# Turning the packed token statistics on VectorE before they are broadcast, in a 16-batch fused embedding and MLP kernel

## The chip, the cores and the metric

The kernel runs on one core of one Trainium2 chip. The metric is the device time of one execution in microseconds; lower is better. One execution was also taken with the hardware profiler, and all rows below are from it.

## The reference

For each of 16 batches, `x` holds 512 tokens of 512 features. Six variants of `x` are built, weighted and concatenated to 3072 features, and go through a two-layer MLP with a layer norm, and the result is added to `x`:

```python
h = _ln(x, pw_g[pathway_ids], pw_b[pathway_ids])
h = _ln(h, cp_g[compartment_ids], cp_b[compartment_ids])
t = _ln(x, tm_g[time_steps], tm_b[time_steps])
m, n, r = (x + _mlp_ln(state_i, ...)[:, None, :] for three state vectors)
s = _ln(x, ms_g[scale_type], ms_b[scale_type])
cat = concatenate([w[0]*h, w[1]*t, w[2]*m, w[3]*n, w[4]*r, w[5]*s], -1)
out = x + _ln(silu(cat @ int_W1 + int_b1) @ int_W2 + int_b2, int_g, int_be)
```

`_ln` normalises over the 512 features of a token. So each token needs its mean and its reciprocal deviation before `t` and `s` can be made.

## The kernel before

All matmuls are exact to about fp32: each operand is split in a high and a low part of type fp32r, and three products (lines 1325 to 1327) are summed in `hid_ps`. Features lie on the partitions and the 512 tokens of a batch in the free dimension: `xc` is `[128, 4, 512]`, transposed `x`. The 16 batches run as `chunk(0)` to `chunk(15)`; chunks 2 to 14 are one hardware loop. The order of the work on each engine is written out by hand, and the engines meet at semaphores.

The statistics of batch b+1 are made while batch b is multiplied. In `x_stats` VectorE takes mean and variance of each token with tokens on the partitions (`xmv`). GpSimd's `x_rstd` turns the variance into the reciprocal deviation, splits it in two fp32r parts and writes `x_pack` `[128 partitions, 2 parts v, 2 statistics s, 4 tokens t]` (lines 452 to 462). The partition p and the number t name the token. But for `t` and `s` the same statistics are needed along the free dimension, on every partition. SyncE's `spread_stats` does this through DRAM: one DMA writes `x_pack` to `token_stats` (line 340), SyncE waits until it has landed, and two DMAs read it back, each to 64 partitions, into `stats_bc` `[128, p, s, t]` (line 347, the first and the second broadcast below). Batch 0 does not use this path; it spreads its statistics with TensorE.

VectorE then uses `stats_bc` in two instructions a batch: `scaled_next` (line 840) multiplies a one-hot mask with the deviations, and `centre` (line 805) subtracts the mean from `xc`. Both read one float in eight: the elements of one statistic are 32 bytes apart.

```python
mean = stats_bc[:, :, 0, :].rearrange("q p t -> q t p").unsqueeze(1).to_broadcast([P, FT, TT, P])
```

TensorE multiplies `scaled` with class tables in `fill(b, j)` (line 1305, into `made_ps`), VectorE multiplies the result with `xc` in `ts_mult(b, j)` (line 854, into `v_ring`), ScalarE and VectorE split that (`ts_high`, `ts_low`, line 859), and TensorE multiplies it with the weights. `fill(b, 0)` waits for `scaled`; `fill(b, 1)` waits for `ts_mult(b, 0)`, as there is one `made_ps`.

The hand-written order of VectorE at the end of a chunk matters here. In chunks 2 to 15 it is: `h_low(b,0)` (line 864), `out_sum(b-1,2)` (line 952), `x_low(b+1,0)` (line 792), `h_low(b,1)`, `out_stats(b-1,3)` (line 904 ff.), `onehot_next`, `scaled_next(b+1)`, two `y_mul` (line 872), `out_sum(b-1,3)`, `x_low(b+1,1)`, `centre(b+1)`, two `y_add` (line 878 ff.), two `y_norm` (line 890), and then `ts_mult(b+1,0)`. In chunk 1 the tail begins with `h_low(1,1)`, `out_sum(0,1)`, `x_low(2,0)`, `out_sum(0,2)`. In chunk 0 it is `y_mul(1,0)`, `y_mul(1,1)`, `add_b1`, `centre(1)`, `scaled_next(1)`, `y_add(1,0)`. `y_norm(b,t)` also needs class rows, which GpSimd gathers with `gather_class(b,t)` (line 490) after `y_mul(b,t)`. SyncE's queue holds, behind `spread_stats(b+1)`, the stores of batch b-1 and the next loads.

Of the kernel before, what the change touches and what calls it, by code (L numbers as in the profile page):

```python
# [7 lines left out]
BATCHES, TOKENS, D = 16, 512, 512  # L8
P = 128
TT = TOKENS // P  # L10
FT = D // P
# [23 lines left out]
def build(nc, x, xT, ids, pid, small, small_at, tm_g, ms_g, rows, net_vecs, pw, cp, W1s, W2s, int_W1, int_W2, out):  # L35
# [4 lines left out]

    x_v = x.rearrange("b (p t) d -> b p t d", t=TT)
    out_v = out.rearrange("b (p t) d -> b p t d", t=TT)
    stats_dram = nc.dram_tensor("token_stats", (2, P, 2 * TT), f32, kind="Internal").ap()

    with ExitStack() as ctx:
        def sb(name, shape, dt=f32):
            return ctx.enter_context(nc.sbuf_tensor(name, shape, dt))

        def sem(name):
            return ctx.enter_context(nc.semaphore(name))  # L50
# [2 lines left out]
        y_sb = sb("y_sb", [P, TT, D])  # L53
        pw_rows = sb("pw_rows", [P, TT, 2 * D])
        xc = sb("xc", [P, FT, TOKENS])
        stats_bc = sb("stats_bc", [P, P, 2, TT])
        r_sb = sb("r_sb", [P, TT, D])
        cat_hi = sb("cat_hi", [P, SLOTS, 2, TOKENS], f32r)
        with ExitStack() as before:
# [49 lines left out]
        xmv = sb("xmv", [P, TT, 2])  # L109
        xve = sb("xve", [P, TT])  # L110
        xrs = sb("xrs", [P, TT])
        x_pack = sb("x_pack", [P, 2, 2, TT])
        split = sb("split", [P, 2, TT])
        split_by = sb("split_by", [P, TT])
        yst = sb("yst", [P, TT, 6])
# [98 lines left out]
        xrs_done = sem("xrs_done")  # L214
        xsplit = sem("xsplit")
        x_packed = sem("x_packed")
        sel_ready = sem("sel_ready")
        mean_diag = sem("mean_diag")
        dev_diag = sem("dev_diag")
# [49 lines left out]
        def wait(eng, s, value):  # L269

            if not isinstance(value, int) or value > 0:
                eng.wait_ge(s, value)
# [40 lines left out]
        def _(sp):  # L313
# [22 lines left out]
                                 ).then_inc((sum_in if j == 0 else sum_more_in)[k], 16)  # L336

            def spread_stats(b):
                sp.wait_ge(x_packed, 4 * b + 2)
                sp.dma_start(stats_dram.rearrange("v p m -> p v m"),  # L340
                             x_pack[:, :, :, :].rearrange("p v s t -> p v (s t)")).then_inc(stats_out, 16)
                sp.wait_ge(stats_out, 16 * b)

                wait(sp, centred, FT * b)
                wait(sp, scaled_ready, b)
                for v in range(2):
                    sp.dma_start(stats_bc[64 * v:64 * v + 64, :, :, :].rearrange("q p s t -> q (p s t)"),
                                 stats_dram[v].rearrange("p m -> (p m)").partition_broadcast(64)
                                 ).then_inc(stats_in[v], 16)

            def store(b, t):
# [82 lines left out]
        def _(pool):  # L434
# [6 lines left out]
            def x_rstd(b):  # L441

                if isinstance(b, int) and b == 1:
                    pool.wait_ge(dev_diag, 1)
                    pool.wait_ge(rest_diag, 1)
                else:
                    wait(pool, stats_out, 16 * (b - 1))
                rstd(xaggr, TT * (b + 1), xve, xve_done, xrs, xrs_done, xmv, slice(0, TT), b + 1)
                pool.nop(nofuse=True)
                if not (isinstance(b, int) and b == 0):  # L450

                    pool.tensor_copy(x_pack[:, 0, 0, :], xmv[:, :, 0]).then_inc(x_packed, 1)
                    pool.tensor_copy(x_pack[:, 1, 0, :], xmv[:, :, 0]).then_inc(x_packed, 1)

                pool.wait_ge(xrs_done, b + 1)
                pool.tensor_tensor(split[:, 0, :], xrs[:, :], split_by[:, :], ALU.mult).then_inc(xsplit, 1)
                pool.wait_ge(xsplit, 2 * b + 1)
                pool.tensor_tensor(split[:, 1, :], split[:, 0, :], xrs[:, :], ALU.subtract).then_inc(xsplit, 1)
                pool.wait_ge(xsplit, 2 * b + 2)
                pool.tensor_tensor(x_pack[:, 0, 1, :], split[:, 0, :], split[:, 1, :], ALU.subtract).then_inc(x_packed, 1)  # L460
                pool.wait_ge(x_packed, 4 * b + 1)
                pool.tensor_tensor(x_pack[:, 1, 1, :], xrs[:, :], x_pack[:, 0, 1, :], ALU.subtract).then_inc(x_packed, 1)
# [52 lines left out]
            pool.memset(minus_half[:, :], -0.5).then_inc(half_ready, 1)  # L515
            pool.memset(eps_col[:, :], EPS).then_inc(half_ready, 1)
            pool.memset(split_by[:, :], 4097.0).then_inc(half_ready, 1)
            pool.memset(net_hidT[:, :, :], 0.0).then_inc(cols_cleared, 1)
            pool.memset(mT[:, :, :], 0.0).then_inc(cols_cleared, 1)
            pool.memset(cat_lo[:, 3, 0, 0:P // 2].bitcast(f32), 1.0).then_inc(sel_ready, 1)  # L520
            pool.memset(cat_lo[:, 3, 0, P // 2:P + P // 2].bitcast(f32), 0.0).then_inc(sel_ready, 1)
            pool.memset(cat_lo[:, 3, 0, P + P // 2:2 * P].bitcast(f32), 1.0).then_inc(sel_ready, 1)
            pool.wait_ge(cols_cleared, 3)
            pool.wait_ge(half_ready, 3)
            pool.wait_ge(sel_ready, 4)
            x_rstd(0)
            pool.wait_ge(row_ids_in, 16)
# [248 lines left out]
        def _(dve):  # L776
# [13 lines left out]
            def x_low(b, i):  # L790
                dve.wait_ge(x_hi_done, 2 * b + i + 1)
                dve.tensor_tensor(cat_lo[:, slot(i), :, :], xc[:, 2 * i:2 * i + 2, :],
                                  cat_hi[:, slot(i), :, :].bitcast(f32), ALU.subtract).then_inc(x_lo_done, 1)

            def stats_here(b):
                for v in range(2):
                    dve.wait_ge(stats_in[v], 16 * b)

            def centre(b):

                dve.wait_ge(x_lo_done, 2 * (b + 1))
                stats_here(b)
                mean = stats_bc[:, :, 0, :].rearrange("q p t -> q t p").unsqueeze(1).to_broadcast([P, FT, TT, P])
                v = xc[:, :, :].rearrange("q f (t p) -> q f t p", t=TT)
                dve.tensor_tensor(v, v, mean, ALU.subtract).then_inc(centred, FT)  # L805

            def centre_tile(f):

# [28 lines left out]
            def scaled_next(b):  # L837
                stats_here(b)
                wait(dve, filled, 6 * (b - 1) + FT)
                dve.scalar_tensor_tensor(scaled[:, :].rearrange("q (t p) -> q t p", t=TT),  # L840
                                         ids_sb[:, :].rearrange("q (t p) -> q t p", t=TT), cls_val[:, 0:1],
                                         stats_bc[:, :, 1, :].rearrange("q p t -> q t p"),
                                         ALU.is_equal, ALU.mult).then_inc(scaled_ready, 1)

            def ts_mult(b, j):
# [210 lines left out]
            def first_chunk():  # L1056
                class_columns()
                x_low(0, 0)
                sum_blocks(0)
                x_stats(0, 0)  # L1060
                sum_low(0)
                x_stats(0, 1)
                x_stats(0, 2)
                x_stats(0, 3)
                sum_blocks(1)
                tab_low()
                sum_low(1)
                x_low(0, 1)
                sum_blocks(2)
                dev_diagonal()  # L1070
                sum_low(2)
                sum_blocks(3)
                scaled_first()
                sum_low(3)
                centre_tile(0)
                ts_mult(0, 0)
                w_low(4)
                w_low(5)
                centre_tile(1)
                ts_low(0, 0)  # L1080
                ts_mult(0, 1)
                w_low(6)
                w_low(7)
                centre_tile(2)
                ts_low(0, 1)
                onehot_first()
                centre_tile(3)
                w_low(8)
                w_low(9)

                dve.wait_ge(tables_ready, 1)
                y_mul(0, 0)
                y_mul(0, 1)
                ts_mult(0, 2)
                y_mul(0, 2)
                y_mul(0, 3)
                ts_low(0, 2)
                w_low(10)
                w_low(11)
                y_add(0, 0)  # L1100
                ts_mult(0, 3)
                y_add(0, 1)
                ts_low(0, 3)
                y_add(0, 2)
                y_add(0, 3)
                w_low(12)
                for t in range(TT):
                    y_norm(0, t)
                w_low(13)
                nets_stats()  # L1110
                h_low(0, 0)
                w_low(14)
                w_low(15)
                x_stats(1, 0)
                h_low(0, 1)
                nets_norm()
                class_rows()
                for t in range(1, TT):
                    x_stats(1, t)
                x_low(1, 0)  # L1120
                nets_weigh()
                x_low(1, 1)
                onehot_next(1)
                y_mul(1, 0)
                y_mul(1, 1)
                add_b1()
                centre(1)
                scaled_next(1)
                y_add(1, 0)

            def chunk(b, last=False):
                if isinstance(b, int) and b == 1:
# [31 lines left out]
                    out_stats(b - 1, 2, o_ps[:, 0, :])  # L1164
                    h_low(b, 1)
                    out_sum(b - 1, 1)
                    x_low(b + 1, 0)
                    out_sum(b - 1, 2)
                else:
# [25 lines left out]
                    out_sum(b - 1, 1)  # L1195
                    out_stats(b - 1, 2, o_ps[:, 0, :])
                    h_low(b, 0)
                    out_sum(b - 1, 2)
                    if not last:
                        x_low(b + 1, 0)  # L1200
# [428 lines left out]
```

## Time and profile before

| | |
|---|---|
| median of 3 runs | 995.85 us (994.02 to 996.64) |
| the profiled execution | 994.5 us, span 992.8 us |
| TensorE busy | 98% of the span |
| VectorE busy | 81% |
| GpSimd busy | 51% |
| ScalarE busy | 27% |
| mean granted TensorE clock | 0.995 |

The span runs from the first to the last instruction; some 1.7 us of the execution lie around it. Busy shares are averages over stages. For a kernel with TensorE at 98% the short list of what TensorE waited for is the first thing to read, and then what stands behind each of these waits.

### The profile page before, as it was taken

What the parts mean: (1) busy time and instruction counts of PE and PEld (TensorE: products, weight loads), DVE (VectorE), ACT (ScalarE), POOL (GpSimd) and SP (SyncE); (2) the same over time, 40 slices, a digit from 0 to 9 for tenths busy, and PEclk for the clock granted to TensorE, in tenths of its full rate; (3) what the DMA queues carried; (4) which work ended last, traced back from release to release, by engine and by line L of the source; (5) the groups of instructions that cost most, each with busy time, mean ns of one, the idle gap of its engine ahead of it and who ended that gap; (6) DMA issues with size and microseconds to landing.
All of it is one profiled execution on the core that took longest, in us unless ns stands there. A gap on an engine that the chain in (4) does not pass through costs nothing.

```text
span 992.8 us, 13724 instructions
## 1 busy us (share of the span) xinstructions
PE 976.8 (98%) x4436; PEld 802.4 (81%) x4436; DVE 800.0 (81%) x1102; ACT 272.1 (27%) x341; POOL 505.4 (51%) x624
## 2 busy tenths in 40 slices
PE   7999999999999999999999999999999999999997
PEld 6677887888888888888888888888888888888885
DVE  6986988697887979878797887879788787987855
ACT  4633232231232322132222312323122232313311
POOL 3442556375554746555374544637445474655322
PEclk9999999999999999999999999999999999999999
DMA  9953546444364553535545363554436355353122
GB/s 317 332 199 117 198 100 191 128 125 143 92 198 98 162 155 82 192 85 179 127 158 139 76 208 85 172 145 127 144 89 206 90 162 153 89 188 86 42 64 64
DMA packets 52738, 141.70 MB, mean 143 GB/s; under 512 B 10200, under 2 KB 10456, under 8 KB 48752
## 3 DMA queue, kind: packets, MB, share of 16 engines
q0 software_dynamic: 22976, 66.07, 26.4%
q1 hardware_dynamic: 29744, 75.41, 21.7%
q8 instruction: 9, 0.15, 0.1%
q14 instruction: 9, 0.07, 0.0%
HBM read 124.55 MB, written 16.90 MB: 142 GB/s over the span
## 4 chain that ended last, share of the span: by engine, by line
PE 84%; DVE 2%; issue 0%; POOL 0%; POOLq 0%; DVEq 0%
PE hid_ps L1327 20%; PE hid_ps L1326 20%; PE hid_ps L1325 20%; PE o_ps L1432 5%; PE o_ps L1431 5%; PE o_ps L1430 5%; PE made_ps L1305 3%; PE made_ps L1318 2%; PE hid_ps L1330 1%; DVE xc L805 0%; PE made_ps L1446 0%; DVE r_sb L943 0%; PE made_ps L1447 0%; PE made_ps L1448 0%; DVE yst L881 0%; DVE fst L927 0%
## 5 line engine op out<-in xcount | busy, mean ns | idle before, releaser
L1325 PE MATMUL hid_ps<-cat_hi,w_hi 128*128 128x512 f32 x1008 | 395.8, 393 | 0.0
L1327 PE MATMUL hid_ps<-cat_hi,w_lo 128*128 128x512 f32 x1008 | 392.9, 390 | 0.0
L1326 PE MATMUL hid_ps<-cat_lo,w_hi 128*128 128x512 f32 x1008 | 392.9, 390 | 0.0
L1325 PEld LDWEIGHTS hid_ps<-cat_hi,w_hi 128*128 128x128 f32 x1008 | 189.7, 188 | 40.1 <-issue 1.7
L1327 PEld LDWEIGHTS hid_ps<-cat_hi,w_lo 128*128 128x128 f32 x1008 | 189.5, 188 | 39.6
L1326 PEld LDWEIGHTS hid_ps<-cat_lo,w_hi 128*128 128x128 f32 x1008 | 189.6, 188 | 38.4
L490 POOL DMA_INDIRECT pw_rows<-cp,class_now x64 | 128.5, 2008 | 66.6 <-DVE y_sb L872 55.2
L659 ACT ACTIVATE cat_hi<-v_ring 128x1024 fp32r<-128x1024 f32 x64 | 68.0, 1062 | 303.3 <-DVE v_ring L854 303.2
L483 POOL DMA_INDIRECT pw_rows<-pw,path_now x64 | 98.4, 1537 | 62.1 <-DVE y_sb L890 41.5
L504 POOL DMA_DIRECT2D r_sb<-x x60 | 57.8, 964 | 109.7 <-DVE r_sb L952 99.0
L437 POOL TENSOR_TENSOR fve<-fmv,eps_col 128x1 f32<-128x1 f32 x64 | 28.5, 445 | 139.4 <-DVE fmv L909 127.1
L1432 PE MATMUL o_ps<-w_lo,hid_hi 128*128 128x512 f32 x240 | 93.4, 389 | 0.0
L1430 PE MATMUL o_ps<-w_hi,hid_hi 128*128 128x512 f32 x240 | 93.4, 389 | 0.0
L1431 PE MATMUL o_ps<-w_hi,hid_lo 128*128 128x512 f32 x240 | 93.4, 389 | 0.0
L859 DVE TENSOR_TENSOR cat_lo<-v_ring,cat_hi 128x1024 fp32r<-128x1024 f32 x64 | 78.3, 1223 | 13.1 <-ACT cat_hi L659 13.1
L674 ACT ACTIVATE z_sb<-hid_ps,batch_bias 128x512 f32<-128x512 f32 x64 | 43.9, 690 | 160.2 <-PE hid_ps L1327 158.6
L664 ACT ACTIVATE cat_hi<-made_ps 128x1024 fp32r<-128x1024 f32 x32 | 32.9, 1027 | 181.0 <-PE made_ps L1318 181.0
L864 DVE TENSOR_TENSOR cat_lo<-made_ps,cat_hi 128x1024 fp32r<-128x1024 f32 x32 | 39.2, 1225 | 51.6 <-ACT cat_hi L664 51.6
L854 DVE TENSOR_TENSOR v_ring<-made_ps,xc 128x1024 f32<-128x1024 f32 x64 | 78.0, 1219 | 2.5 <-PE made_ps L1305 2.5
L904 DVE TENSOR_TENSOR o_sb<-o_ps,rows_bc 128x512 f32<-128x512 f32 x60 | 41.1, 685 | 44.3 <-PE o_ps L1432 44.3
L805 DVE TENSOR_TENSOR xc<-xc,stats_bc 128x2048 f32<-128x2048 f32 x15 | 61.2, 4078 | 5.7 <-DMA stats_bc<-token_stats 4.4
L890 DVE SCALAR_TENSOR_TENSOR y_sb<-y_sb,ymv,pw_rows 128x512 f32<-128x512 f32 x64 | 46.3, 747 | 18.7 <-DMA pw_rows<-cp,class_now 18.7
(157 smaller groups left out, 1239.2 us busy)
## 6 DMA issues: line engine op xcount, KB each, us to landing
x_sb<-x SPq DMA_DIRECT2D x16, 1024.0 KB, 6.3
out<-r_sb SPq DMA_DIRECT2D x64, 256.0 KB, 2.0
xc<-xT SPq DMA_DIRECT2D x15, 1024.0 KB, 5.0
r_sb<-x POOLq DMA_DIRECT2D x60, 256.0 KB, 4.8
stats_bc<-token_stats SPq DMA_DIRECT2D x30, 256.0 KB, 5.2
ids_sb<-ids SPq DMA_DIRECT2D x16, 256.0 KB, 7.3
keep<-int_W SPq DMA_DIRECT2D x12, 256.0 KB, 7.1
w_raw<-int_W SPq DMA_DIRECT2D x12, 256.0 KB, 10.6
```

The lines of the kernel that those rows point to most:

```text
L483: pool.indirect_dma_start(pw_rows[:, t, :], None, pw[:, :], bass.IndirectOffsetOnAxis(ap=path_now[:, t:t + 1], axis=0)).then_inc(rows_in[t ...
L490: pool.indirect_dma_start(pw_rows[:, t, 0:D], None, cp[:, :], bass.IndirectOffsetOnAxis(ap=class_now[:, t:t + 1], axis=0)).then_inc(class_ ...
L659: act.activation(cat_hi[:, slot(TS0 + j), :, :], v_ring[:, slot(TS0 + j), :, :], ACT.Copy).then_inc(ts_hi_done, 1)
L805: dve.tensor_tensor(v, v, mean, ALU.subtract).then_inc(centred, FT)
L854: dve.tensor_tensor(v_ring[:, slot(TS0 + j), :, :], made_ps[:, :, :], xc[:, j:j + 1, :].to_broadcast([P, 2, TOKENS]), ALU.mult).then_inc(v ...
L859: dve.tensor_tensor(cat_lo[:, slot(TS0 + j), :, :], v_ring[:, slot(TS0 + j), :, :], cat_hi[:, slot(TS0 + j), :, :].bitcast(f32), ALU.subtr ...
L1325: pe.matmul(acc, w1_hi[:, k, cols], hi, start=start, stop=False)
L1326: pe.matmul(acc, w1_hi[:, k, cols], lo, start=False, stop=False)
L1327: return pe.matmul(acc, w1_lo[:, k, cols], hi, start=False, stop=stop)
L1430: pe.matmul(acc, hid_hi[:, k, cols], w2_hi[:, k, :], start=(k == 0), stop=False)
L1431: pe.matmul(acc, hid_lo[:, k, cols], w2_hi[:, k, :], start=False, stop=False)
L1432: ins = pe.matmul(acc, hid_hi[:, k, cols], w2_lo[:, k, :], start=False, stop=(k == FT - 1))
```

## The change

VectorE's 32 by 32 square transpose turns the pack before it leaves. `x_pack` becomes a view of the first 16 columns of `pack_cols` `[128, 32]` (the other 16 are cleared once); `turn_stats` transposes each square of 32 partitions by 32 columns into `pack_rows`. Partition 32g+m then holds value m (one of v, s, t) of 32 tokens. Four DMAs of 16 rows by 32 floats write that to `token_stats`, now `[32, 128]`, where it had been one DMA of 128 partitions by 2 pieces of 8 floats. The two broadcasts move the same bytes as before, but `stats_bc` is now `[128, s, 512 tokens]`, so `centre` and `scaled_next` read it without gaps. SyncE now waits for `pack_turned`, so for VectorE, where it had waited for GpSimd.

```diff
-    stats_dram = nc.dram_tensor("token_stats", (2, P, 2 * TT), f32, kind="Internal").ap()
+    stats_dram = nc.dram_tensor("token_stats", (32, P), f32, kind="Internal").ap()
-        stats_bc = sb("stats_bc", [P, P, 2, TT])
+        stats_bc = sb("stats_bc", [P, 2, TOKENS])
-        x_pack = sb("x_pack", [P, 2, 2, TT])
+        pack_cols = sb("pack_cols", [P, 32])
+        pack_rows = sb("pack_rows", [P, 32])
+        x_pack = pack_cols[:, 0:4 * TT].rearrange("p (v s t) -> p v s t", v=2, s=2)
...
             def spread_stats(b):
-                sp.wait_ge(x_packed, 4 * b + 2)
-                sp.dma_start(stats_dram.rearrange("v p m -> p v m"),
-                             x_pack[:, :, :, :].rearrange("p v s t -> p v (s t)")).then_inc(stats_out, 16)
-                sp.wait_ge(stats_out, 16 * b)
+                sp.wait_ge(pack_turned, b)
+                for g in range(P // 32):
+                    sp.dma_start(stats_dram[0:4 * TT, 32 * g:32 * g + 32], pack_rows[32 * g:32 * g + 4 * TT, :]
+                                 ).then_inc(stats_out, 16)
+                sp.wait_ge(stats_out, 64 * b)
...
                 for v in range(2):
-                    sp.dma_start(stats_bc[64 * v:64 * v + 64, :, :, :].rearrange("q p s t -> q (p s t)"),
-                                 stats_dram[v].rearrange("p m -> (p m)").partition_broadcast(64)
+                    sp.dma_start(stats_bc[64 * v:64 * v + 64, :, :].rearrange("q s j -> q (s j)"),
+                                 stats_dram[2 * TT * v:2 * TT * (v + 1), :].rearrange("m p -> (m p)").partition_broadcast(64)
                                  ).then_inc(stats_in[v], 16)
...
-                    wait(pool, stats_out, 16 * (b - 1))
+                    wait(pool, pack_turned, b - 1)
...
+            pool.memset(pack_cols[:, 4 * TT:32], 0.0).then_inc(half_ready, 1)
...
+            def turn_stats(b):
+                dve.wait_ge(x_packed, 4 * b + 2)
+
+                wait(dve, stats_out, 64 * (b - 1))
+                dve.transpose(pack_rows[:, :], pack_cols[:, :]).then_inc(pack_turned, 1)
+
...
-                mean = stats_bc[:, :, 0, :].rearrange("q p t -> q t p").unsqueeze(1).to_broadcast([P, FT, TT, P])
-                v = xc[:, :, :].rearrange("q f (t p) -> q f t p", t=TT)
-                dve.tensor_tensor(v, v, mean, ALU.subtract).then_inc(centred, FT)
+                mean = stats_bc[:, 0:1, :].to_broadcast([P, FT, TOKENS])
+                dve.tensor_tensor(xc[:, :, :], xc[:, :, :], mean, ALU.subtract).then_inc(centred, FT)
...
-                dve.scalar_tensor_tensor(scaled[:, :].rearrange("q (t p) -> q t p", t=TT),
-                                         ids_sb[:, :].rearrange("q (t p) -> q t p", t=TT), cls_val[:, 0:1],
-                                         stats_bc[:, :, 1, :].rearrange("q p t -> q t p"),
+                dve.scalar_tensor_tensor(scaled[:, :], ids_sb[:, :], cls_val[:, 0:1], stats_bc[:, 1, :],
                                          ALU.is_equal, ALU.mult).then_inc(scaled_ready, 1)
```

`turn_stats` stands in VectorE's order in three places: in chunk 0 ahead of `add_b1`, in chunk 1 ahead of `x_low(2, 0)`, and in chunks 2 to 14 behind `h_low(b, 0)`.

## Rows read from the trace of the kernel before

**Rows 1.** What TensorE waited for behind batch 0: us, times, longest us.

```profile
PE made_ps L1305 <- DVE v_ring L854: 2.0, 1, 2.0
PE made_ps L1305 <- DVE scaled L840: 1.2, 1, 1.2
```

**Rows 2.** Stretches of TensorE: length, busy (instructions), granted clock, DMA share, GB/s.

```profile
92.10:98.00 5.90, 5.90 (x26) 1.00 0.00 0
...
153.80:157.30 3.50, 3.50 (x9) 0.52 0.43 108
```

**Rows 3.** A later period: PE, PEld, DVE, ACT, POOL busy, clock, DMA share, GB/s.

```profile
212.52:271.44 58.92, 58.92 (x269) 48.94 (x269) 48.34 (x66) 15.42 (x18) 32.50 (x39) 1.00 0.47 138
```

**Rows 4.** Timeline of batch 1, VectorE: start, length, instruction, idle before and releaser.

```profile
86.76 4.06 DVE L805 TENSOR_TENSOR xc<-xc,stats_bc 128x2048 f32<-128x2048 f32 x1 [4.45 <-DMA stats_bc<-token_stats]
90.74 1.14 DVE L840 SCALAR_TENSOR_TENSOR scaled<-ids_sb,small_sb,stats_bc 128x512 fp32r<-128x512 int32 x1
```

**Rows 5.** The same of TensorE, the fill that waited in batch 2.

```profile
153.71 1.22 PE L1305 MATMUL made_ps<-scaled,class_tab 128*128 128x512 f32 x2 [2.03 <-DVE v_ring L854]
```

**Rows 6.** Timeline of VectorE ahead of the wait in batch 2.

```profile
131.55 0.74 DVE L952 SCALAR_TENSOR_TENSOR r_sb<-o_sb,frs,rows_bc 128x512 f32<-128x512 f32 x1
...
139.32 1.22 DVE L840 SCALAR_TENSOR_TENSOR scaled<-ids_sb,small_sb,stats_bc 128x512 fp32r<-128x512 int32 x1 [0.96 <-issue]
...
143.75 4.11 DVE L805 TENSOR_TENSOR xc<-xc,stats_bc 128x2048 f32<-128x2048 f32 x1
...
151.10 1.41 DVE L890 SCALAR_TENSOR_TENSOR y_sb<-y_sb,ymv,pw_rows 128x512 f32<-128x512 f32 x2
```

**Rows 7.** SyncE's DMA issues: two at the start, the statistics of batches 2 and 7.

```profile
4.40 0.37 SPq L373 DMA_DIRECT2D y_sb<-tm_g  x1
4.82 0.37 SPq L374 DMA_DIRECT2D y_sb<-ms_g  x1
...
131.14 0.38 SPq L340 DMA_DIRECT2D token_stats<-x_pack  x1
132.71 1.24 SPq L347 DMA_DIRECT2D stats_bc<-token_stats  x2
...
424.04 1.11 SPq L347 DMA_DIRECT2D stats_bc<-token_stats  x2
```

**Rows 8.** Landing of the two broadcasts in batches 1, 2 and 7, after their issue.

```profile
DMA to landing us min/median/max: 5.1/6.2/7.2
...
DMA to landing us min/median/max: 4.0/5.0/6.0
...
DMA to landing us min/median/max: 4.6/4.9/5.2
```

**Rows 9.** VectorE's groups by form: busy us, mean ns, idle before.

```profile
L792 DVE TENSOR_TENSOR cat_lo<-xc,cat_hi 128x1024 fp32r<-128x1024 f32 x32 | 39.0, 1220 | 1.5 <-ACT cat_hi L655 1.5
...
L811 DVE TENSOR_TENSOR xc<-xc,o_ps 128x512 f32<-128x512 f32 x4 | 2.7, 680 | 0.0
...
L820 DVE SCALAR_TENSOR_TENSOR scaled<-ids_sb,small_sb,o_ps 128x512 fp32r<-128x512 int32 x1 | 0.8, 750 | 1.4 <-PE o_ps L1374 1.4
...
L1005 DVE CAST class_cols<-small_sb 128x20 fp32r<-128x20 f32 x6 | 0.6, 174 | 0.0
```

**Rows 10.** Timeline of a later period: VectorE's tail and the fill behind it.

```profile
424.63 1.22 DVE L864 TENSOR_TENSOR cat_lo<-made_ps,cat_hi 128x1024 fp32r<-128x1024 f32 x1 [2.53 <-ACT cat_hi L664]
...
435.39 1.22 DVE L840 SCALAR_TENSOR_TENSOR scaled<-ids_sb,small_sb,stats_bc 128x512 fp32r<-128x512 int32 x1
...
448.47 1.22 DVE L854 TENSOR_TENSOR v_ring<-made_ps,xc 128x1024 f32<-128x1024 f32 x1
...
450.07 0.61 PE L1305 MATMUL made_ps<-scaled,class_tab 128*128 128x512 f32 x2
```

**Rows 11.** GpSimd's second gather of class rows for batch 2, and its landing after issue.

```profile
144.96 3.75 POOL L490 DMA_INDIRECT pw_rows<-cp,class_now  x1 [0.30 <-issue]
...
DMA to landing us min/median/max: 5.9/5.9/5.9
```

More of the change, by code:

```diff
@@ L216, in build @@
         x_packed = sem("x_packed")
+        pack_turned = sem("pack_turned")
         sel_ready = sem("sel_ready")
@@ L523, in _ @@
             pool.wait_ge(cols_cleared, 3)
-            pool.wait_ge(half_ready, 3)
+            pool.wait_ge(half_ready, 4)
             pool.wait_ge(sel_ready, 4)
@@ L1125, in first_chunk @@
                 y_mul(1, 1)
+                turn_stats(1)
                 add_b1()
@@ L1166, in chunk @@
                     out_sum(b - 1, 1)
+                    turn_stats(b + 1)
                     x_low(b + 1, 0)
@@ L1197, in chunk @@
                     h_low(b, 0)
+                    if not last:
+                        turn_stats(b + 1)
                     out_sum(b - 1, 2)
```

## The prediction

> **What bounds the kernel now.** I read the waits of TensorE first, then its stretches, then the timelines of VectorE, SyncE and GpSimd around each wait. Behind the prologue TensorE waits twice in the whole run: 1.2 us in batch 1 for `scaled`, and 2.0 us in batch 2 for `ts_mult` [rows 1]. From batch 3 on there is nothing left: the period is 58.92 us and TensorE is busy for all of it, at full clock [rows 3]. So in 13 of the 15 batches that the change touches, faster work of VectorE buys nothing; what it can buy lies in those two waits and in what they do to the clock. After the second wait the granted clock is 0.52 for 3.5 us, the lower level of 1.2 GHz; after the first it stays at 1.00, 2.4 GHz [rows 2]. The 3.5 us at about half clock hold work of about 1.8 us, so the fall costs some 1.6 to 1.7 us. Most that can be won is then 1.2 + 2.03 + 1.65 = 4.9 us [rows 1, 5, 2].
>
> What stands behind each wait is the path of the statistics. In batch 1 VectorE sits idle 4.45 us until the broadcasts land at 86.76, then does `centre` and `scaled_next` to 90.74 + 1.14 = 91.88, which releases TensorE's fill [rows 4, 1]. In batch 2 VectorE is idle 0.96 us before `scaled_next` at 139.32; the view names no releaser, but the second broadcast, issued near 133.25 with a landing of 6.0 us, arrives at about 139.3, so it is that. From there VectorE runs without a gap through `centre` and two `y_norm`, that end at 151.10 + 1.41 = 152.5, and `ts_mult` behind them; the fill follows at 153.71 [rows 6, 7, 8, 5].
>
> **What VectorE gains in each batch.** `centre` takes 4.06 to 4.11 us for 2048 elements [rows 4, 6]. A tensor_tensor without gaps takes 680 ns for 512 elements and 1220 ns for 1024 [rows 9], so 540 ns for 512 more, and 2048 elements come to 1220 + 2 x 540 = 2300 ns: 1.8 us less. Lower end: nothing is gained if the gaps are not what makes it slow; upper end 1.8. `scaled_next` takes 1.14 to 1.22 us [rows 4, 10]; the same instruction of batch 0 reads its statistics from `dev_ps` without gaps in 750 ns [rows 9]: 0.45 less. Together 2.25 us a batch, all on the path from the landing to the fills; I take it whole, since the instruction of batch 0 differs in nothing but the operand.
>
> **What the way to DRAM loses.** Four things are added ahead of the broadcasts.
> The transpose itself has no row. The nearest small instruction, a cast of 20 columns, takes 174 ns [rows 9]; a full 512 columns take 680 [rows 9]. I take 0.2 us, since 32 columns are near 20; the bounds are 0.17 and 0.7.
> It is queued on VectorE. In chunk 0 VectorE is idle at that place (part of the wait for `add_b1`), so nothing waits. In chunk 1 it stands behind `out_sum(0,1)`, which ends at 131.55 + 0.74 = 132.29, where the write had been issued at 131.14 [rows 6, 7]: 1.15 us later, and with the transpose 1.35. In later chunks it stands behind `h_low(b,0)`, which ends at 424.63 + 1.22 = 425.85, while the write there was issued some 1.57 us ahead of the broadcasts at 424.04, so near 422.47: 3.4 us later, 3.6 with the transpose [rows 10, 7].
> Four DMAs are issued where one was. SyncE starts small ones 0.42 us apart (4.40, 4.82) [rows 7], so the last goes out 3 x 0.42 = 1.25 us after the first. From issue of the write to the next issue SyncE now needs 132.71 - 131.14 = 1.57 us [rows 7]. I keep 1.57 for the last of the four: fewer and larger pieces may take less, but GpSimd's add of x runs beside them now, which may cost more. Bounds: 1.2 and 2.5.
> Behind SyncE's longer wait stand the stores and, in chunk 0, the load of `rows_bc`; both are needed far later. On VectorE, `x_low` stands behind the transpose in chunk 1 and is then followed by an idle wait, which hides 0.2 us. In later chunks the transpose falls into the tail's idle time ahead of `h_low(b,1)`.
> The cleared columns are written in the prologue, where GpSimd waits for VectorE anyway: nothing. GpSimd's `x_rstd` waits for the transpose of the batch before, long done.
>
> The Trainium skill, "DMA: Bandwidth & Descriptors", section "Anatomy of one DMA", puts the fixed cost of a DMA at about 2.0 us, most of it until the write is confirmed. By it the last write would take some 0.4 us longer than the 1.57 of the trace, and the sum below would lose that much in each of the two waits, so about 0.5 us less gain in all, as the second wait has hardly a gain to lose before it turns into a loss. It was fitted to the other kind of queue, and the row decides.
>
> **Sum for batch 1.** The broadcasts go out 0.2 + 1.25 = 1.5 us later (1.1 to 2.5 by the bounds above). They land 5.1 to 7.2 us after issue, slower than elsewhere [rows 8], since gathers and other loads share the engines; issued later they meet less of the gathers, so I take 1.2 us later. 2.25 - 1.2 = 1.05 us earlier for `scaled`, of a wait of 1.2: gain 1.05, with bounds of 1.15 and 0. All engines then run earlier by as much, as VectorE is busy without a long gap up to batch 2.
>
> **Sum for batch 2.** The broadcasts go out 1.35 + 1.25 = 2.6 us later, the second near 135.85. With the 6.0 us of this batch it lands at 141.85, with the 5.2 of a later one at 141.05 [rows 8]: 1.7 to 2.55 us later than 139.3. I take 2.1, between. The wait becomes 2.03 + 2.1 - 2.25 = 1.9 us, gain 0.15; by the bounds it is 1.5 to 2.4. Close to the old wait, so I leave the fall of the clock where it is.
>
> The gather of class rows is on this way too, as `y_norm` needs it. Its second instruction takes 3.75 us, begins beside `centre` and ends at 148.71, 0.85 us after it [rows 6, 11]. I read it as held up by `centre`, so it ends earlier with it and does not become the new wait. The Trainium skill, "SBUF — State Buffer", section "Who interferes with whom", says that a tensor_tensor with two SBUF inputs contends with GpSimd's reads and infers that descriptor writing is not held up by it; by that the gather stays where it is in relation to `y_mul`, and its rows would come too late by some of what `centre` saves. The row leans the other way; the case is rival four.
>
> **The later batches.** The second broadcast, issued near 424.55, landed at 429.75, 5.6 us ahead of `scaled_next` at 435.39 [rows 7, 8, 10]. It goes out 3.6 + 1.25 = 4.85 us later and lands near 434.6: still 0.8 us ahead. Beyond that, `scaled_next` may be late by the 2.25 us saved and by the slack of `ts_mult`: 448.47 + 1.22 = 449.69, where TensorE comes to the fill at 450.07, 0.38 us [rows 10]. So TensorE waits only if the landing slips another 0.8 + 2.25 + 0.4 = 3.4 us. Cost here: nothing, gain nothing.
>
> **Total.** 1.05 + 0.15 = 1.2 us. The profiled execution would go from 994.5 to 993.3; the median of the runs is 1.35 us above it, so 995.85 becomes about 994.7. A measurement of this kernel can tell a change from none at about 0.3%, 3.0 us; this is 0.12%.
>
> **The rivals.**
> One, chance 0.54: as above, 993.9 to 995.6.
> Two, the clock: both waits shrink so far that the clock stays up. The trace has a wait of 1.2 us without a fall and one of 2.03 with it; between these I can't tell. It takes a batch 2 landing at or below the lower bound. Gain 1.1 + 0.6 + 1.65 = 3.35, up to 4.9: 992.5, at best 991.0. Chance 0.22, of which a bit over three quarters lie beyond 0.3%.
> Three, nothing: the later landing eats all in both places, because the writes take 2.5 us or the broadcasts are as slow as in batch 1. 995.8, chance 0.1.
> Four, the gather becomes the wait: it landed 5.9 us after 144.96, at 150.85, and the second `y_norm` began in the middle of its pair, near 151.8, 0.95 later [rows 11, 6]. If it isn't tied to `centre`, 1.8 - 0.95 = 0.85 us of the gain are lost in batch 2: wait 2.75, total gain 0.35, so 995.5. Chance 0.05.
> Five, slower: SyncE's new chain is too late in the 13 later batches. It decides from 3.4 us beyond my landing; each further us costs 13 us, as every period is bound by TensorE. At 1 us over: 1009. For it speaks that its chain grows by 4.85 us of 5.6; against it that the landings spread over little more than 3 us. Chance 0.05.
> Six, the change does not do what it says: `centre` stays at 4.1 us as the broadcast operand, not the gap, makes it slow. Then both waits grow by 1.2 and 2.1 us: 999.2. Against it, `ts_mult` also reads a repeated operand and takes 1.22 us for 1024 elements [rows 10]. Chance 0.04.
>
> **How the numbers follow.** Faster by over 0.3%: 0.17 from rival two, and 0.02 from noise of rival one. Slower: 0.05 + 0.04, and 0.01 of noise. The rest, 0.71, is within 0.3%. The range takes the best of the clock case, 4.9 us with little off, and on the other side the case of nothing with the spread of the runs (1.3 us): 991.4 to 997.2. Beyond it lie rivals five and six and little else.
>
> **What would show it.** `centre` near 2.3 us and `scaled_next` near 0.75; a transpose of about 0.2; four issues at 0.3 to 0.42 us; the broadcasts of batch 1 landing near 88.0, of batch 2 some 2.1 us later against `out_sum(0,1)` than before; in TensorE's list of waits 0.2 us in batch 1, 1.9 us in batch 2, none later; and a period still of 58.92. I am wrong if the wait of batch 2 is gone (clock at 1.00 there), or if waits for `scaled` or `v_ring` appear in every period.

## The result

The changed kernel takes 998.25 us (median of 20 runs, 995.12 to 1000.11) against 994.66 us (20 runs, 992.50 to 996.64) for the kernel before, measured beside it. The ratio is 1.0037, with a 95% interval of 1.0029 to 1.0045: 3.7 us slower, where 1.2 us faster was forecast, and above the range that ended at 997.2. The span of the profiled execution went from 992.8 to 997.2 us.

TensorE's waits behind batch 0 in the changed kernel (us in total, times, longest) are the same two as in [rows 1], and both have grown:

```profile
PE made_ps L1319 <- DVE v_ring L864: 3.7, 1, 3.7
PE made_ps L1319 <- DVE scaled L852: 2.2, 1, 2.2
```

Stretches behind the two waits, and one later period (length, busy, clock, DMA share, GB/s; the period with all engines):

```profile
93.10:98.50 5.40, 5.38 (x17) 0.68 0.00 0
150.00:158.10 8.10, 4.38 (x20) 1.00 0.42 97
158.10:162.80 4.70, 4.68 (x13) 0.64 0.54 160
...
448.20:507.10 58.90, 58.90 (x270) 48.93 (x269) 46.29 (x67) 15.40 (x19) 30.25 (x39) 1.00 0.47 137
```

The later period is as full as that of [rows 3]. But now the clock also falls behind the wait of batch 1, where it had stayed up at a wait of 1.2 us [rows 2]. A fall costs the stretch times what is missing of the clock: 5.40 x 0.32 = 1.73 us there, and 4.70 x 0.36 = 1.69 in batch 2, against 3.50 x 0.48 = 1.68 in [rows 2]. The 4.4 us of span are then all accounted for: the first wait 2.2 - 1.2 = 1.0, the new fall 1.7, the second wait 3.75 - 2.03 = 1.7, the old fall the same as before.

The two longer waits and the new fall make up the loss; they do not yet say why the waits grew. VectorE did what it was meant to. Its groups by form (busy us, mean ns, idle before) have `centre` at 2.29 us, `scaled_next` at 0.74 and the transpose at 0.20, against 4.06 to 4.11 and 1.14 to 1.22 in [rows 4, 6]:

```profile
L817 DVE TENSOR_TENSOR xc<-xc,stats_bc 128x2048 f32<-128x2048 f32 x15 | 34.4, 2292 | 8.8 <-DMA stats_bc<-token_stats 7.6
L852 DVE SCALAR_TENSOR_TENSOR scaled<-ids_sb,small_sb,stats_bc 128x512 fp32r<-128x512 int32 x15 | 11.2, 743 | 6.2 <-issue 6.2
L806 DVE STREAM_TRANSPOSE pack_rows<-pack_cols 128x32 f32<-128x32 f32 x15 | 3.0, 202 | 0.6 <-POOL pack_cols L468 0.6
```

The loss is on the way to DRAM. SyncE's issues of batch 1 in the kernel before:

```profile
77.31 0.39 SPq L340 DMA_DIRECT2D token_stats<-x_pack  x1
78.90 1.10 SPq L347 DMA_DIRECT2D stats_bc<-token_stats  x2
```

And in the changed kernel, in batches 1, 2 and 7:

```profile
77.69 1.71 SPq L346 DMA_DIRECT2D token_stats<-pack_rows  x4
82.48 1.10 SPq L353 DMA_DIRECT2D stats_bc<-token_stats  x2
...
135.17 2.55 SPq L346 DMA_DIRECT2D token_stats<-pack_rows  x4
140.18 1.09 SPq L353 DMA_DIRECT2D stats_bc<-token_stats  x2
...
430.43 1.73 SPq L346 DMA_DIRECT2D token_stats<-pack_rows  x4
433.16 1.10 SPq L353 DMA_DIRECT2D stats_bc<-token_stats  x2
```

From the first write to the broadcasts SyncE needs 4.8 us in batch 1 and 5.0 in batch 2, but 2.7 in batch 7 (1.6 in batch 1 before), where I had expected 1.25 + 1.57 = 2.8 everywhere. The landings of the writes, in batch 1 (all four), batch 2 (the first three, with how long their issue took: min, median, max in ns) and batch 8 (the first two; all four give the same row), say why:

```profile
DMA to landing us min/median/max: 1.3/1.4/3.5
...
L346 SPq DMA_DIRECT2D token_stats<-pack_rows x3: 324/422/1255, 135.2 to 136.8; - x3
...
DMA to landing us min/median/max: 2.4/3.0/4.2
...
DMA to landing us min/median/max: 1.3/1.4/1.4
```

A write of 2 KB lands in 1.4 us where it is alone. In batch 1 the last one, issued at 78.98, takes 3.5. GpSimd begins its gathers right beside the writes (its timeline: start, length), and between 79.0 and 82.4 us, while the last write is under way, GpSimd's software queue keeps the DMA engines 72.9% busy:

```profile
77.95 1.05 POOL L489 DMA_INDIRECT pw_rows<-pw,path_now  x1 [0.53 <-issue]
...
q0 software_dynamic: 181, 0.68, 72.9%
q1 hardware_dynamic: 85, 0.01, 1.6%
```

In the kernel before the one write of batch 1 was through by 78.90, ahead of these transfers. In batch 2 it is GpSimd's add of x that starts beside the writes, at 135.57. The packets (the pieces in which a DMA moves its data) show where the writes stood. A 2 KB write has 32 of them, in the hardware queue. In batch 1 none moved from 79.65 to 81.20, while GpSimd's queue kept the engines 86.7% busy; those of the last write moved between 81.4 and 82.0 us, 2.4 to 3.0 us after its issue, where those of the first had moved 0.8 to 1.0 us after theirs. In batch 2 the queues from 138.0 and from 138.5 us, half a microsecond each, were

```profile
q0 software_dynamic: 38, 0.08, 89.3%
...
q0 software_dynamic: 48, 0.09, 95.5%
q1 hardware_dynamic: 36, 0.00, 6.0%
```

and 60 more packets of the hardware queue moved from 139.0 on. So the 96 packets of the last three writes moved only when GpSimd's burst, which had begun at 137.2, came to its end.

In batch 2 one issue also took 1.26 us in place of 0.42; a load of instructions falls in the same half microsecond. Batch 3 has the same: there an issue took 1.69 us and a write up to 4.5 to land, the longest of all 60 writes (issue in ns, then landing):

```profile
L346 SPq DMA_DIRECT2D token_stats<-pack_rows x60: 324/420/1686, 77.7 to 903.1; - x60
...
DMA to landing us min/median/max: 1.3/1.4/4.5
```

SyncE needed 5.7 us in batch 3, and still TensorE did not wait. Two theories follow. Theory C (collision): the last of four writes is issued late enough to run beside GpSimd's transfers, and SyncE waits for the last. Rival L: the turn on VectorE, or rows of 128 bytes, is what makes the path slow.

### The profile page after: what moved, and what is told of

Same layout as the page of the kernel before. It is cut to its first block, busy times and chain, and to the rows that moved or that the text cites. A ratio compares the mean times of both kernels' runs of the same rounds, so it can differ in the third digit from the quotient of the medians.

```text
span 997.2 us, 13773 instructions
## 1 busy us (share of the span) xinstructions
PE 976.6 (98%) x4436; PEld 801.9 (80%) x4436; DVE 768.4 (77%) x1117; ACT 272.4 (27%) x341; POOL 476.5 (48%) x625
## 4 chain that ended last, share of the span: by engine, by line
PE 83%; DVE 1%; issue 0%; POOL 0%; POOLq 0%; DVEq 0%
PE hid_ps L1341 20%; PE hid_ps L1340 20%; PE hid_ps L1339 20%; PE o_ps L1446 5%; PE o_ps L1445 5%; PE o_ps L1444 5%; PE made_ps L1319 3%; PE made_ps L1332 2%; PE hid_ps L1344 1%; DVE xc L817 0%; PE made_ps L1460 0%; DVE r_sb L953 0%; PE made_ps L1461 0%; PE made_ps L1462 0%; DVE yst L891 0%
## 5 line engine op out<-in xcount | busy, mean ns | idle before, releaser
L496 POOL DMA_INDIRECT pw_rows<-cp,class_now x64 | 103.2, 1612 | 66.5 <-DVE y_sb L882 55.0
L443 POOL TENSOR_TENSOR fve<-fmv,eps_col 128x1 f32<-128x1 f32 x64 | 25.0, 391 | 137.5 <-DVE fmv L919 125.2
L443 POOL TENSOR_TENSOR yve<-ymv,eps_col 128x1 f32<-128x1 f32 x64 | 40.0, 626 | 43.0 <-DVE ymv L894 43.0
```

Of the source, the lines that this page charges most:

```text
L443: pool.tensor_tensor(ve[:, cols], mv[:, cols, 1], eps_col[:, cols], ALU.add).then_inc(ve_sem, 1)
L496: pool.indirect_dma_start(pw_rows[:, t, 0:D], None, cp[:, :], bass.IndirectOffsetOnAxis(ap=class_now[:, t:t + 1], axis=0)).then_inc(class_ ...
```

## The experiments

Each kernel was timed beside the kernel before, whose median was 994.23 us for the first four and 994.19 for the others.

**One write.** All 128 rows of `pack_rows` go out in one DMA; the turn and the rows of 128 bytes stay.

```diff
-                for g in range(P // 32):
-                    sp.dma_start(stats_dram[0:4 * TT, 32 * g:32 * g + 32], pack_rows[32 * g:32 * g + 4 * TT, :]
-                                 ).then_inc(stats_out, 16)
-                sp.wait_ge(stats_out, 64 * b)
+                sp.dma_start(stats_dram.rearrange("m (g j) -> g m j", j=32), pack_rows[:, :]).then_inc(stats_out, 16)
+                sp.wait_ge(stats_out, 16 * b)
...
-                wait(dve, stats_out, 64 * (b - 1))
+                wait(dve, stats_out, 16 * (b - 1))
```

> The changed kernel with one DMA of all 128 partitions in place of the four of 16. Theory C (collision): the time was lost because the last of four writes is issued 1.3 us late and then runs beside the transfers of GpSimd's DMAs (the gathers in batch 1, the add of x in batch 2), where it takes 3.5 to 4.2 us to land and not 1.4. One write goes out ahead of them: from its issue to the broadcasts 1.5 to 1.8 us in both batches, the wait for scaled in batch 1 at most 0.3 us, the wait for v_ring in batch 2 from 2.0 down to about 1.3, and a time 1 to 4 us below the kernel before. Rival L (layout or turn): writes of transposed rows are slow by themselves, or VectorE's place in the chain costs the time: then only the 1.3 us of issue come back in each place, the broadcasts still go out 3.5 us behind the write, and the time stays 1 to 3 us above the kernel before.

991.37 us, ratio 0.9971 (0.9959 to 0.9983): faster than the kernel before. SyncE's issues in batches 1 and 2, and TensorE's two waits:

```profile
77.64 0.62 SPq L345 DMA_DIRECT2D token_stats<-pack_rows  x1
79.68 1.15 SPq L351 DMA_DIRECT2D stats_bc<-token_stats  x2
...
131.72 0.57 SPq L345 DMA_DIRECT2D token_stats<-pack_rows  x1
133.70 1.12 SPq L351 DMA_DIRECT2D stats_bc<-token_stats  x2
...
PE made_ps L1317 <- DVE scaled L850: 0.4, 1, 0.4
PE made_ps L1317 <- DVE v_ring L862: 0.3, 1, 0.3
```

The path takes 2.0 us in both batches, with the same turn and the same rows. So rival L falls, and the four writes carry the loss. The path is a little longer than the 1.8 us that I gave it, the first wait with 0.4 us longer than the 0.3, and the second shorter than the 1.3 us.

**The reads alone.** The kernel before with its old write; only `centre` and `scaled_next` read `stats_bc` without gaps. The order of the values is left out, so the statistics reach the wrong tokens.

```diff
-                mean = stats_bc[:, :, 0, :].rearrange("q p t -> q t p").unsqueeze(1).to_broadcast([P, FT, TT, P])
...
+                flat = stats_bc[:, :, :, :].rearrange("q p s t -> q (p s t)")
+                mean = flat[:, 0:TOKENS].unsqueeze(1).to_broadcast([P, FT, TOKENS])
...
-                                         stats_bc[:, :, 1, :].rearrange("q p t -> q t p"),
...
+                dve.scalar_tensor_tensor(scaled[:, :], ids_sb[:, :], cls_val[:, 0:1], flat[:, TOKENS:2 * TOKENS],
...
```

> The kernel before with its old way through DRAM, where centre and scaled_next read the same bytes without gaps (so the statistics reach the wrong tokens; the order of the values is left out). Both theories: centre 2.29 us, scaled_next 0.75, both of TensorE's waits behind batch 0 gone or below 0.3 us, the clock stays at 1.00 after batch 2, and 4 to 5 us below the kernel before: the whole price of the change then lies in the way to DRAM. Rival G (the class gather is not tied to centre): a wait of 0.6 to 1 us stays in batch 2. Rival P: the gain would be taken from every period, 1.8 us in each of 15 batches, 25 us or more.

989.27 us, ratio 0.9947 (0.9930 to 0.9965), 5.0 us below the kernel before. In the stretch over both places (length, busy, clock, DMA share, GB/s) TensorE never stops:

```profile
85.00:155.00 70.00, 70.00 (x318) 1.00 0.48 145
```

This is the whole worth of contiguous reads, and it agrees with the bound of 4.9 us in the prediction. Rivals G and P fall: no wait behind batch 0 is left, and 5.0 us in all are far from a gain in every period.

**The path alone.** The changed kernel, with reads in the old pattern. Again only the order of the values is left out.

```diff
-                mean = stats_bc[:, 0:1, :].to_broadcast([P, FT, TOKENS])
+                old = stats_bc[:, :, :].rearrange("q s j -> q (s j)").rearrange("q (p s t) -> q p s t", s=2, t=TT)
+                mean = old[:, :, 0, :].rearrange("q p t -> q t p").unsqueeze(1).to_broadcast([P, FT, TT, P])
...
```

> The changed kernel (turn on VectorE, four writes), where centre and scaled_next read with the old gaps of 32 bytes (so the wrong values; the order is left out). If the two parts add up: waits of 2.2 + 2.25 = 4.4 us in batch 1 and 3.75 + 2.25 = 6.0 in batch 2, none in later batches, and some 8 to 9 us above the kernel before. If the later landing also touches the later periods, as scaled_next has only about 1 us to spare there, waits of up to 1 us appear in 13 batches and the time is 10 to 20 us above.

1005.82 us, ratio 1.0112 (1.0087 to 1.0137). TensorE's waits:

```profile
PE made_ps L1324 <- DVE v_ring L869: 6.1, 2, 5.8
PE made_ps L1324 <- DVE scaled L855: 3.9, 1, 3.9
```

The long waits are near the sum of the parts (4.4 and 6.0 expected). The second wait for `v_ring` is one of 0.3 us in batch 3; from batch 4 on there is none. The time, 11.6 us above the kernel before, is more than the 8 to 9 expected, because the falls of the clock behind the longer waits are longer. Stretches around the two:

```profile
95.00:105.00 10.00, 9.37 (x29) 0.66 0.00 0
...
163.00:172.00 9.00, 8.05 (x23) 0.62 0.56 188
```

Each costs 10.00 x 0.34 or 9.00 x 0.38, so 3.4 us, twice that of the changed kernel. I had put no price on that.

**GpSimd behind the writes.** The changed kernel with its four writes; GpSimd waits for their landing ahead of the gathers of batch 1 and of the add of x in batch 2.

```diff
+                if first:
+                    pool.wait_ge(stats_out, 64)
                 if not last:
                     gather(b + 1, 2)
...
+                    if isinstance(b, int) and b == 1:
+                        pool.wait_ge(stats_out, 128)
                     add_x(b - 1, 1)
```

> The changed kernel with all four writes, but GpSimd waits until they have landed before it starts the gathers for batch 1 and the add of x beside batch 2's writes. Theory C: each write lands in 1.3 to 1.4 us, the broadcasts go out 2.7 us behind the first write in both batches, the wait in batch 1 is below 1 us, that in batch 2 near 2, the time within 2 us of the kernel before. Rival L: the last write still takes 3 us or more with nothing beside it, and the time stays 3 to 4 us above the kernel before.

993.48 us, ratio 0.9988 (0.9977 to 1.0000). SyncE's issues and the landing of the writes in batch 1, then the issues of batch 2, an instruction queue's share in the half microsecond from 131.0, and what is left of TensorE's waits:

```profile
77.73 1.73 SPq L346 DMA_DIRECT2D token_stats<-pack_rows  x4
80.46 1.10 SPq L353 DMA_DIRECT2D stats_bc<-token_stats  x2
...
DMA to landing us min/median/max: 1.3/1.4/1.4
...
131.14 2.88 SPq L346 DMA_DIRECT2D token_stats<-pack_rows  x4
135.02 1.09 SPq L353 DMA_DIRECT2D stats_bc<-token_stats  x2
...
q8 instruction: 1, 0.02, 16.6%
...
PE made_ps L1323 <- DVE v_ring L868: 2.7, 1, 2.7
```

Batch 1 shows the collision cleanly: with GpSimd held, all four land in 1.4 us and the path takes 2.7. The wait for `scaled` is gone; here the broadcasts gain too, as they also run without the gathers (3.9 us to landing, 5.8 to 6.9 in the changed kernel), so the size of this gain is not the writes' alone. Batch 2 came out above the 2.7 us expected, at 3.9, with the last two writes landing in 1.4: the rest is an issue that took 1.6 us, again beside a load of instructions, beside which the first two writes took 2.6 to 2.8 us to land. That is a second cause in batch 2, which the theory did not have; its wait of 2.7 us is above the 2 expected.

**TensorE kept busy.** The changed kernel with matmuls that nobody reads in the two waits. For TensorE `chunk(2)` is taken out of the hardware loop, so that only batch 2 has the second group.

```diff
+            def keep_busy(n):
+                for i in range(n):
+                    pe.matmul(o_ps[:, 1, :], w1_hi[:, 0, 0:P], w1_hi[:, 1, :], start=True, stop=True)
...
                     first_pair(b)
+                    keep_busy(8)
                     fill(b, 0)
...
                     first_pair(b)
+                    if isinstance(b, int) and b == 2:
+                        pe.wait_ge(o_done, TT)
+                        keep_busy(13)
                     fill(b, 1)
...
+            chunk(2)
...
```

> The changed kernel with matmuls of two weight tiles into an unused bank of o_ps, put in TensorE's two waits: 8 ahead of fill(1,0) and 13 ahead of fill(2,1), 0.23 us each, so 1.8 and 3.0 us of work that nobody reads where TensorE was idle for 2.2 and 3.75. Theory C: some 3 us of the cost of the waits is the fall of the clock behind them, because TensorE had been idle; with the fillers the clock stays at 1.00 behind both, the idle time before the fills is 0.4 and 0.8 us, the fills start at the same time as in the changed kernel, and 3 us come back, so about the time of the kernel before. Rival: the fall comes from something else than the idle time (then it stays, and so does the time).

995.73 us, ratio 1.0021 (1.0012 to 1.0030). The stretches behind the two fills, as in the changed kernel above:

```profile
93.20:98.60 5.40, 5.40 (x25) 1.00 0.00 0
...
156.40:161.10 4.70, 4.63 (x20) 1.00 0.51 153
```

The clock stays up behind both, so the falls do come from the idle time. The fill of batch 1 starts at 93.06 (93.12 in the changed kernel), so the fillers delay nothing there. The gain is 2.5 us between the medians and 1.6 between the ratios, less than the 3 us expected; the span fell by 3.2.

This profile also parts the two causes in batch 2, since here no issue was slow and no load of instructions ran beside the writes. The issues of batch 2 and the landing of its writes:

```profile
133.48 1.71 SPq L346 DMA_DIRECT2D token_stats<-pack_rows  x4
138.16 1.10 SPq L353 DMA_DIRECT2D stats_bc<-token_stats  x2
...
DMA to landing us min/median/max: 1.3/1.4/3.4
```

The last write alone takes 3.4 us and the path 4.7, against 5.0 in the changed kernel. So the add of x accounts for 2.0 us of the 2.3 by which the path of batch 2 is above 2.7; the slow issue added some 0.3.

**Four writes without the turn.** The kernel before, with its write cut in four of 32 partitions.

```diff
-                sp.dma_start(stats_dram.rearrange("v p m -> p v m"),
-                             x_pack[:, :, :, :].rearrange("p v s t -> p v (s t)")).then_inc(stats_out, 16)
-                sp.wait_ge(stats_out, 16 * b)
+                for g in range(4):
+                    sp.dma_start(stats_dram[:, 32 * g:32 * g + 32, :].rearrange("v p m -> p v m"),
+                                 x_pack[32 * g:32 * g + 32, :, :, :].rearrange("p v s t -> p v (s t)")
+                                 ).then_inc(stats_out, 16)
+                sp.wait_ge(stats_out, 64 * b)
...
```

> The kernel before with nothing changed but the write: four DMAs of 32 partitions of x_pack in place of one of 128, no transpose, reads with gaps. It parts the number of writes from the turn on VectorE. Theory C: the last write is issued at about 78.6 in batch 1, 0.4 us earlier than in the changed kernel, at the edge of the gathers' transfers: broadcasts 1.3 to 3 us later than before, in batch 2 about 1.5 to 2.5 later; waits of 2.5 to 4 us each, no wait in later batches, 3 to 7 us above the kernel before. Rival L (the turn on VectorE or the transposed rows are what costs): the write still lands 1.6 us after its last issue, the waits grow by 1.3 us each at most, and the time is 2.5 to 3 us above.

1000.35 us, ratio 1.0070 (1.0056 to 1.0084). SyncE's issues of batch 1 and TensorE's waits:

```profile
77.05 1.76 SPq L341 DMA_DIRECT2D token_stats<-x_pack  x4
82.20 1.10 SPq L349 DMA_DIRECT2D stats_bc<-token_stats  x2
...
PE made_ps L1307 <- DVE scaled L842: 3.8, 1, 3.8
PE made_ps L1307 <- DVE v_ring L856: 3.1, 1, 3.1
```

The number of writes alone, without turn or transposed rows, makes the path 5.2 us long in batch 1. In batch 4, with no load of instructions near, its last write takes 3.4 us too and the path 4.7. So neither the turn nor the rows of rival L are needed for the loss.

**Two steps further.** One write, and the turn of batch 2 ahead of `out_sum(0,1)`:

```diff
                     h_low(b, 1)
+                    turn_stats(b + 1)
                     out_sum(b - 1, 1)
-                    turn_stats(b + 1)
```

> The kernel with one write, and in chunk 1 the turn ahead of out_sum(0,1) in VectorE's order, not behind it. Theory C: the write of batch 2 goes out 0.5 to 0.7 us earlier, the wait of 0.3 us for v_ring goes; at most 0.3 us below one_write, not told apart by the median. Rival: out_sum and with it the add of x is 0.2 us later, nothing else changes.

991.57 us, ratio 0.9977 (0.9967 to 0.9987), not told apart from one write. In its profile both waits are 0.8 us, where I expected the second to go: the broadcasts took 7.0 to 8.2 us in batch 1 and 5.6 to 6.0 in batch 2, against 6.7 to 7.8 and 4.2 to 4.8 with one write. Batch 1 is the same in the two kernels, so part of this is chance; whether the earlier write of batch 2 has a part in its slower landing is not shown. The same, and the gathers of batch 1 behind the one write (`pool.wait_ge(stats_out, 16)` in chunk 0):

> The same, and GpSimd starts the two gathers of batch 1 only when the write has landed. Theory C: in batch 1 the broadcasts share the engines with less, land 2 to 3 us earlier (near 85 to 86), and the last wait of 0.4 us in batch 1 goes too; no wait behind batch 0 is left, and the time comes to that of the kernel where only the reads changed, 989 to 990.5 us against 994.2 before. Rival: the gathers, started 1.3 us later, delay the first y_mul or y_norm of batch 1 and give it back; then nothing is gained against one_write_early.

990.63 us, ratio 0.9970 (0.9959 to 0.9980). In batch 1 the two broadcasts land in

```profile
DMA to landing us min/median/max: 3.6/3.8/4.1
```

and only batch 2's wait is left, 0.7 us, where I expected none and 989 to 990.5 us. It has the lowest median of the versions that keep the order of the values, but its interval overlaps with that of one write alone.

## Why the prediction was wrong

The step that failed is "I keep 1.57 for the last of the four", with the bounds 1.2 and 2.5. The last write took 3.5 us in batch 1 and 2.9 in batch 2. The text even named the traffic ("GpSimd's add of x runs beside them now, which may cost more"), but only for batch 2, and bounded it at 2.5 without a row. The bounds did not carry even that: in batch 1 the upper ones add up to 0.7 + 1.25 + 0.93 = 2.9 us later, not 2.5, and in batch 2 the 2.4 us of wait leave out the 0.93 by which the write might be late. For batch 1 the prediction looked for what the gathers do to the broadcasts, not to a write of 2 KB, though by its own sum that write now fell among them. The second step that failed is a term put at nothing: the sum for batch 1 has no fall of the clock, since its worst case there was no gain; a fall stood only in batch 2, as one that might go. The fall in batch 1 cost 1.7 us.

Point by point:

- **The bound of the kernel.** Right. Two waits and the clock behind them hold all that this change can move: 5.0 us were won with the reads alone, and from batch 4 on TensorE waits in none of the kernels.
- **VectorE's gain.** Right: 2.29 + 0.74 us against 2.30 + 0.75 forecast.
- **The transpose.** 0.20 us as forecast, beside idle time of VectorE in the three places where it stands.
- **Issue of four writes.** 1.71 us for four, 0.43 each, as forecast; in batches 2 and 3 wrong by 0.8 and 1.3 us, as one issue took 1.26 and 1.69.
- **Batch 1.** The broadcasts went out 3.6 us later, not 1.5, and landed 3.3 later, not 1.2. Less the 2.25 us saved, the wait grew by 1.0 where it should have shrunk by 1.05. That wait of 2.2 us then brought down the clock, 1.7 us more.
- **Batch 2.** Against the end of `out_sum(0,1)` the broadcasts went out 140.18 - 135.02 = 5.2 us after it, against 132.71 - 132.29 = 0.4 before: 4.7 later, not 2.6. Of the excess of 2.1 us, 0.8 are the slow issue and 1.3 the landing; but TensorE kept busy shows that without the slow issue the write would have met the same burst, and only 0.3 us would have been saved. They then landed 0.7 us faster; the wait grew by 1.7.
- **Later batches.** Right from batch 4 on: writes land in 1.4 us, the path takes 2.7, and no wait appears. In batch 3 the path took 5.7 us, and TensorE did not wait there either. `scaled_next` of batch 7 starts at 439.85, some 1.2 us behind the landing.
- **The gather.** The reading in the trace held. In batch 2 of the changed kernel GpSimd's second gather and `centre` are

```profile
151.19 1.93 POOL L496 DMA_INDIRECT pw_rows<-cp,class_now  x1 [0.30 <-issue]
...
149.99 2.29 DVE L817 TENSOR_TENSOR xc<-xc,stats_bc 128x2048 f32<-128x2048 f32 x1
```

so the gather ends at 153.12, 0.84 us behind `centre`, as it ended 0.85 us behind the longer one [rows 6, 11]. With `centre` 1.8 us shorter the gather is 1.8 us shorter. The Trainium skill, "SBUF — State Buffer", section "Who interferes with whom", infers that descriptor writing is not held up by a tensor_tensor. This trace leans against that: the gather took 3.75 us beside the centre of 4.11 and 1.93 beside that of 2.29, but 0.97 in batch 1 without one. That section of the Trainium skill also says that a tensor_tensor with two SBUF inputs contends with what GpSimd reads from SBUF. The trace does not part the two. The cause of the tie was not tried by itself.

What a rule on landing would have given: the Trainium skill, "DMA: Bandwidth & Descriptors", section "Latency and other measured facts", says that access to HBM takes 0.2 us on average and 2 us at high load, and that this is the main part of a DMA's fixed cost. The difference measured here between a write alone and one among the gathers, 3.5 - 1.4 = 2.1 us, is of that size, but the packets place it: it had passed before the last packet moved, 3.0 us after the issue against 1.0, and the landing followed that packet within 0.5 us in both cases. So it is not shown to be a slower access to the memory. An estimate by that page's figures, 1.57 + 1.8 = 3.4 us as the upper bound in place of 2.5, would have put a loss in batch 1 within the bounds.

What stays open: why the write's packets are held while GpSimd's run, and why they then move at the end of the burst in batch 2 but at 81.4 us in batch 1, with GpSimd's queue still busy. They may queue behind its packets in the DMA engines, or their own reads may be held up; no run here parts the two.

## What to carry to other kernels

Price a DMA that others wait for by what runs beside it at its new time, not by its landing at the old one; a write cut in four lands when its last part does, and each part is another chance to meet a burst of traffic. When a wait ahead of a saturated TensorE may grow past one that kept the clock up, add the fall of the clock to its price. And when a change trades VectorE's time for a longer way through DRAM, time the two halves apart: here the reads alone were worth -5.0 us and the path with four writes alone +11.6, and one write in place of four kept over half of the gain.

## What the runs showed of the hardware

- The landing of a 2 KB write to DRAM took 1.3 to 1.4 us alone, and 3.4 to 3.5 us for the last of four that met GpSimd's transfers (batch 1; batch 2 with TensorE kept busy). It took 2.6 to 2.8 us beside a load of instructions with GpSimd held, and up to 4.5 with both. A write of 8 KB in 128 partitions by 2 pieces took 1.6 us alone.
- In batch 1 no packet of the hardware queue moved for 1.55 us while GpSimd's queue kept the engines 86.7% busy.
- Reading one float in eight (32 bytes apart) cost `centre` 4.06 to 4.08 us against 2.29 without gaps, and `scaled_next` 1.21 against 0.74.
- The clock stayed at its upper level (2.4 GHz) behind waits of TensorE of 0.3 to 1.2 us here and fell to the lower one (1.2 GHz) for parts of the next microseconds behind waits of 2.0 to 5.8 us; unread matmuls in the wait kept it up.
- In the three profiles with four writes of `pack_rows` other than that with TensorE kept busy, one of SyncE's four issues took 1.1 to 1.7 us in place of 0.4 in batch 2 and again in batch 3. Each of these six began within 0.2 us of the start of a load of instructions; no other issue of a write was slow, and the nearest loads beside four writes that left them alone started 0.23 and 0.30 us behind an issue.
